# Expert attention on one NeuronCore: the order of a step's projections, the place and form of the routing, the split of the values

## The chip, the cores and the metric

The kernel runs on one core of one Trainium2 chip. The metric is the time of the whole program on the device in microseconds (us), median of the runs.

## What is computed

Eight blocks follow one another, each adding its output to the residual stream of 2 x 1024 tokens by 128 channels. The change concerns the block `_L1_ffn_ref`, which runs twice (stages `g0_` and `g1_`). The reference, cut to it:

```python
def _L1_ffn_ref(x, Wq, Wkv, Ws, Wd, Wo):
    H, E, DH, K = (8, 5, 64, 3)
    ss = sigmoid(x @ Ws).reshape(b, t, H, E);  sd = sigmoid(x @ Wd).reshape(b, t, H, E)
    ms = _topk_mask(ss, K);  md = _topk_mask(sd, K)
    ss_g = ss * ms;  sd_g = sd * md
    q5 = (x @ Wq).reshape(b, t, H, E, DH)
    kv = (x @ Wkv).reshape(b, t, 2, H, E, DH)
    q = einsum('bthed,bthe->bhtd', q5, sd_g)
    k = einsum('bthed,bthe->bhtd', kv[:, :, 0], ss_g)
    v = einsum('bthed,bthe->bhtd', kv[:, :, 1], ss_g)
    attn = softmax(einsum('bhid,bhjd->bhij', q * scale, k), axis=-1)
    out = einsum('bhij,bhjd->bihd', attn, v)
    o5 = einsum('bthd,dm->bthm', out, Wo).reshape(b, t, H, E, DIM)
    return einsum('bthem,bthe->btm', o5, md)
```

Each head's queries, keys and values are sums over five experts weighted by gates; the output of a head is handed to the experts that the mask `md` keeps.

## The kernel before

`expert_attention_stage` walks through 8 units (a pair of heads of one batch entry), each of T = 8 steps: step j handles 128 query rows against 1024 keys for the two heads, so there are STEPS = 64 steps, t = j % T. The five engines each run a list of instructions written out by hand and meet at semaphores; the class `HeadStream` holds what belongs to one step.

In a step TensorE makes the scores of the next step (`scores`, L1505: 4 matmuls of 128 x 512), turns the last 256 columns of head 0's probabilities (`transpose`, L1516) and later subtracts their bf16 part (`subtract`, L1525), and multiplies the probabilities of the step before with the values (`values`, L1546, 24 matmuls of 65 columns for each head, in bf16 parts). Between these it projects tokens for steps to come (`project`, L2292): `beside(k)`, for k = 0, 1, 2, issues two matmuls of 320 columns into the banks 6 and 7, for values (eight steps ahead), queries and keys (eleven ahead). There is only this pair of banks, so `beside` first waits until VectorE has multiplied the products before by the gates (`product_ready`). At t = 2 and 6 TensorE also turns the next unit's queries and keys (`turn`, L2298), and ScalarE places them.

VectorE in a step: the two row maxima (`dve_max`, L1595), three products with the gates (`apply_gates`; L2589 for queries, L2592 for keys and values), two sums over experts (`sum_values`, L2599; `sum_keys`, L2606), and the routing of the step before (`dve_route`): a reciprocal of the row sums (L1602), its product with the mask (`share`, L1604), and the product of outputs and share for 2 heads x 5 experts x 64 (L1608). GpSimd adds what was routed into `z` (`route`, L2479 to L2482) at the end of its step, after the low parts of the probabilities (`pool_lo`, L1582) and the sum over the queries' experts (`sum_queries`, L2491 to L2493). SyncE issues two DMA transposes a step, of the high and the low part (L1591).

At a unit's first step (t = 0) the unit's values are split into two bf16 parts in one piece: ScalarE casts 1040 columns (`act_split_values`, L1614), VectorE subtracts (`dve_split_values`, L1618), before it may write the next unit's values over them.

```python
if j + 1 < STEPS:
    hs.dve_max(dve, j + 1, 0)
beside(0)
if j + 1 < STEPS:
    hs.dve_max(dve, j + 1, 1)
...
beside(1)
if t == 0 and unit:
    hs.dve_split_values(dve, unit)
if j + T < TOTAL:
    sum_values(j + T)
if j:
    route(j - 1)
beside(2)
```

The loop for VectorE stands above. In the first 53 steps of a stage all three projections are there; in steps 53 to 55 only that for values, in the last unit none, and there the results are projected out instead (`turn_out`, `project_out`).

Of the kernel before, what the change touches and what calls it, by code (L numbers as in the profile page):

```python
# [14 lines left out]
ALU = mybir.AluOpType  # L15
# [3 lines left out]
P = 128  # L19
# [1425 lines left out]
class HeadStream:  # L1445
# [8 lines left out]
    def __init__(self, core, ctx, tag, sums):  # L1454
# [16 lines left out]
        self.share = sb("share", [P, 2, 5])  # L1471
# [11 lines left out]
        self.recip_ready, self.share_ready = sem("recip_ready"), sem("share_ready")  # L1483
# [43 lines left out]
    def values(self, pe, j, h):  # L1527
        b = j // self.T % 2
        self.wait_turned(pe, j)
        if h == 0:  # L1530
            pe.wait_ge(self.r_split, j + 1)
            if j:
                pe.wait_ge(self.o_ready, j)
            if j % self.T == 0:
                pe.wait_ge(self.v_split, j // self.T + 1)
# [62 lines left out]
    def dve_route(self, dve, j, kept, added):  # L1598
# [5 lines left out]
        self.nc.vector.tensor_tensor(self.share[:], kept, self.core.col(self.recip[:], 5), ALU.mult).then_inc(self.share_ready, 1)  # L1604
        dve.wait_ge(self.share_ready, j + 1)
        if j >= 2:
            dve.wait_ge(added, j - 1)
        self.nc.vector.tensor_tensor(self.routed[:, j % 2], o[:, :, 0:64].unsqueeze(2).to_broadcast([P, 2, 5, 64]),  # L1608
                                     self.share[:].unsqueeze(3).to_broadcast([P, 2, 5, 64]), ALU.mult).then_inc(self.o_ready, 1)

    def act_split_values(self, act, unit, ready):
# [543 lines left out]
def expert_attention_stage(core, tag):  # L2155
# [10 lines left out]
    with ExitStack() as ctx:  # L2166
# [96 lines left out]
        def _(pe):  # L2263
# [74 lines left out]
            for j in range(STEPS):  # L2338
# [18 lines left out]
                beside(0)  # L2357
# [7 lines left out]
                beside(1)  # L2365
# [7 lines left out]
                beside(2)  # L2373
# [13 lines left out]
        def _(act):  # L2387
# [48 lines left out]
            hs.act_split_values(act, 0, (v_ready, T))  # L2436
            for j in range(STEPS):
# [10 lines left out]
                if t == 0 and unit:  # L2448
                    hs.act_split_values(act, unit, (v_ready, (unit + 1) * T))
# [15 lines left out]
        def _(pool):  # L2465
# [57 lines left out]
            for j in range(STEPS):  # L2523
# [8 lines left out]
                if j:  # L2532
# [4 lines left out]
        def _(dve):  # L2537
# [111 lines left out]
            for tile in range(T, LEAD):  # L2649
# [720 lines left out]
```

## Time and profile before

| | |
|---|---|
| median of 3 runs | 2662.1 us (2661.57 to 2664.65) |
| the profiled execution, its own time | 2660.86 us |
| its span | 2659.0 us |
| PE busy | 2357.8 us (89%) |
| DVE busy | 2034.9 us (77%) |
| ACT busy | 1478.0 us (56%) |
| POOL busy | 1783.3 us (67%) |
| first and last L1559 in g0_ and g1_ (all x256) | 1389.9 to 2630.1 us |

PE is TensorE's matmuls, DVE VectorE, ACT ScalarE, POOL GpSimd. A row of the timeline gives start, duration and instruction, and in brackets how long the engine had been idle before and who ended that. Matmuls are pipelined, so from one group to the next the starts tell what the group costs, and the printed duration is somewhat longer; the same holds for VectorE, whose next instruction starts before the printed end of the last.

### The profile page before, as it was taken

What the parts mean: (1) busy time and instruction counts of PE and PEld (TensorE: products, weight loads), DVE (VectorE), ACT (ScalarE), POOL (GpSimd) and SP (SyncE); (2) the same over time, 40 slices, a digit from 0 to 9 for tenths busy, and PEclk for the clock granted to TensorE, in tenths of its full rate; (3) what the DMA queues carried; (4) which work ended last, traced back from release to release, by engine and by line L of the source; (5) the groups of instructions that cost most, each with busy time, mean ns of one, the idle gap of its engine ahead of it and who ended that gap; (6) DMA issues with size and microseconds to landing.
All of it is one profiled execution on the core that took longest, in us unless ns stands there. A gap on an engine that the chain in (4) does not pass through costs nothing. (4 is left out here: it accounts for less than half of the span.)

```text
span 2659.0 us, 55314 instructions
## 1 busy us (share of the span) xinstructions
PE 2357.8 (89%) x21054; PEld 1521.2 (57%) x21054; DVE 2034.9 (77%) x3668; ACT 1478.0 (56%) x2069; POOL 1783.3 (67%) x1676
## 2 busy tenths in 40 slices
PE   6788777887799999999979999999879799999987
PEld 3555534644466666666655666665634466666655
DVE  7998545545677777777679999998577999999983
ACT  4222122332788888888924556665653255566564
POOL 0888200000899999999947888888710478888885
PEclk9899779988899999999989999999989999999997
DMA  1000000001699998989924656666610256666665
GB/s 45 1 1 0 1 24 14 1 24 53 117 166 148 158 160 151 161 152 154 150 83 87 112 110 114 112 114 118 124 32 0 70 112 112 112 112 115 116 119 107
DMA packets 829351, 243.47 MB, mean 92 GB/s; under 512 B 811528, under 2 KB 820232, under 8 KB 829088
## 3 DMA queue, kind: packets, MB, share of 16 engines
q1 hardware_dynamic: 829088, 239.93, 49.0%
q8 instruction: 168, 2.75, 0.4%
q14 instruction: 95, 0.78, 0.1%
HBM read 20.70 MB, written 1.05 MB: 8 GB/s over the span
## 5 line engine op out<-in xcount | busy, mean ns | idle before, releaser
L2292 PE MATMUL banks<-g_w,normed_t 128*128 128x320 f32 x1536 | 508.3, 457 | 47.8 <-DVE g_scratch L2592 34.0
L1582 POOL TENSOR_TENSOR g_p_lo<-g_p,g_p_hi 128x768 bf16<-128x768 f32 (+1 forms) x256 | 478.2, 1889 | 34.9 <-POOL g_z L2482 22.3
L1775 DVE TENSOR_REDUCE at_negmax<-banks 128x1 f32<-128x1024 f32 x256 | 301.6, 1220 | 152.9 <-PE banks L1687 152.9
L2292 PEld LDWEIGHTS banks<-g_w,normed_t 128*128 128x128 f32 x1536 | 261.6, 189 | 237.6 <-DVE g_scratch L2592 115.0
L1752 POOL TENSOR_TENSOR at_p_lo<-at_p,at_p_hi 128x640 bf16<-128x640 f32 x256 | 356.1, 1408 | 13.4 <-ACT at_p_hi L1740 11.7
L1595 DVE TENSOR_REDUCE g_negmax<-banks 128x1 f32<-128x1024 f32 x256 | 310.1, 1217 | 40.7 <-PE banks L1505 40.5
L1559 ACT ACTIVATE g_p<-banks,g_negmax 128x1024 f32<-128x1024 f32 x256 | 284.9, 1113 | 9.1 <-DVE g_negmax L1595 8.8
L1733 ACT ACTIVATE at_p<-banks,at_negmax 128x1024 f32<-128x1024 f32 x256 | 285.4, 1115 | 6.3 <-DVE at_negmax L1775 6.3
L1687 PE MATMUL banks<-at_k_t,at_q 64*128 64x512 f32 x1024 | 257.0, 620 | 18.1 <-POOL at_k_t L2036 10.0
L1505 PE MATMUL banks<-g_k_t,g_q 64*128 64x512 f32 x1024 | 256.2, 619 | 16.9 <-ACT g_p L1559 10.4
L1572 ACT CAST g_r_hi<-banks 128x256 bf16<-128x256 f32 x128 | 47.6, 372 | 396.5 <-PE banks L1516 396.5
L1566 ACT CAST g_p_hi<-g_p 128x768 bf16<-128x768 f32 (+1 forms) x256 | 241.7, 944 | 6.9 <-DMA g_t_lo<-g_p_lo 2.9
L2592 DVE TENSOR_TENSOR g_scratch<-banks,g_gate 128x640 f32<-128x640 f32 x256 | 209.5, 819 | 5.0 <-PE banks L2292 1.4
L1546 PE MATMUL banks<-g_v_hi,g_t_hi 128*128 128x65 bf16 x1792 | 193.8, 195 | 15.1 <-DMA g_t_lo<-g_p_lo 15.0
L1546 PE MATMUL banks<-g_v_lo,g_t_hi 128*128 128x65 bf16 x1792 | 193.9, 195 | 0.0
L1546 PE MATMUL banks<-g_v_hi,g_t_lo 128*128 128x65 bf16 x1792 | 192.9, 195 | 0.0
L1740 ACT CAST at_p_hi<-at_p 128x640 bf16<-128x640 f32 x256 | 185.9, 726 | 7.7
L1759 POOL TENSOR_TENSOR at_u_lo<-at_u 128x768 bf16<-128x768 f32 x128 | 188.1, 1470 | 2.3 <-ACT at_u L1746 1.6
L1546 PEld LDWEIGHTS banks<-g_v_hi,g_t_hi 128*128 128x128 bf16 x1792 | 167.5, 98 | 34.2 <-DMA g_t_lo<-g_p_lo 20.0
L1546 PEld LDWEIGHTS banks<-g_v_lo,g_t_hi 128*128 128x128 bf16 x1792 | 167.3, 99 | 2.8
L1546 PEld LDWEIGHTS banks<-g_v_hi,g_t_lo 128*128 128x128 bf16 x1792 | 167.5, 99 | 0.0
L1505 PEld LDWEIGHTS banks<-g_k_t,g_q 64*128 64x128 f32 x1024 | 88.8, 187 | 129.3 <-issue 96.0
(419 smaller groups left out, 5996.0 us busy)
## 6 DMA issues: line engine op xcount, KB each, us to landing
at_swapped<-at_crossed SPq DMA_DIRECT2D x128, 128.0 KB, 2.7
g_w<-in_ex_w SPq DMA_DIRECT2D x2, 2880.0 KB, 11.5
f_w<-in_W SPq DMA_DIRECT2D x2, 1024.0 KB, 5.6
at_rope<-in_rope SPq DMA_DIRECT2D x1, 2048.0 KB, 9.6
at_t_hi<-at_p_hi SPq DMA_TRANSPOSE x128, 3.6
at_t_lo<-at_p_lo SPq DMA_TRANSPOSE x128, 3.6
g_t_hi<-g_p_hi SPq DMA_TRANSPOSE x128, 4.2
g_t_lo<-g_p_lo SPq DMA_TRANSPOSE x128, 4.2
```

Source lines behind the costliest of these rows:

```text
L1505: ins = self.nc.tensor.matmul(self.core.ps[2 * h + half], self.q[rows, b, t * P:(t + 1) * P], self.kt[rows, b, half * CHUNK:(half + 1) * C ...
L1546: ins = self.nc.tensor.matmul(self.sums[:, at:at + 65], p, v[:, b, k, h, :], start=(k == 0 and i == 0), stop=(k == self.T - 1 and i == 2))
L1559: self.nc.scalar.activation(self.p[:, j % 2, h, :], self.core.banks[:, 2 * h:2 * h + 2, :], ACT.Exp, bias=self.negmax[:, h:h + 1]).then_in ...
L1566: self.nc.scalar.copy(self.part(self.p_hi, j, h), self.p[:, j % 2, h, 0:self.WIDTH[h]]).then_inc(self.hi_ready, 1)
L1582: self.nc.gpsimd.tensor_tensor(self.part(self.p_lo, j, h), self.p[:, j % 2, h, 0:self.WIDTH[h]], self.part(self.p_hi, j, h), ALU.subtract) ...
L1595: self.nc.vector.tensor_reduce(self.negmax[:, h:h + 1], self.core.banks[:, 2 * h:2 * h + 2, :], AX.XY, ALU.max, negate=True).then_inc(self ...
L1687: ins = self.nc.tensor.matmul(self.core.ps[self.pair(j, h) + half], self.q[rows, b, t * P:(t + 1) * P], self.kt[rows, b, half * CHUNK:(hal ...
L1733: self.nc.scalar.activation(self.p[:, j % 2, h, :], self.core.banks[:, first:first + 2, :], ACT.Exp, bias=self.negmax[:, j % 2, h:h + 1]). ...
L1752: self.nc.gpsimd.tensor_tensor(self.p_lo[:, j % self.RING, h, :], self.p[:, j % 2, h, 0:self.BY_DMA * P], self.p_hi[:, j % self.RING, h, : ...
L1775: self.nc.vector.tensor_reduce(self.negmax[:, j % 2, h:h + 1], self.core.banks[:, first:first + 2, :], AX.XY, ALU.max, negate=True).then_i ...
L2292: nc.tensor.matmul(out[:, 0:ED], core.xt[:, at:at + P], w[:, kind * H + tile // (T * BATCH) * 2 + h, :], start=True, stop=True).then_inc(p ...
L2592: v.tensor_tensor((k_product if kind == 1 else v_product)[:, tile % 2], src.rearrange("p h (c e) -> p h c e", e=E), own.unsqueeze(2).to_br ...
```

## The change

It touches only the two stages of expert attention.

- Projections: `beside(0)` now comes before the scores on TensorE, `beside(1)` behind them, `beside(2)` between the products with the values. On VectorE they stand accordingly: `beside(0)` at the step's start, `beside(1)` between the two maxima, `beside(2)` after them.
- Routing: from j = 2 to j = 56 step j routes step j - 2, right behind `beside(0)`, and GpSimd adds the same step; from j = 56 on step j - 1 is routed at the old place (step 56 does both). `share` is gone: each head is one instruction with a scalar and two tensors, (output x reciprocal) x mask, over 5 x 64.
- Values: split in two halves of four tiles, the first at t = 4 of the unit before, the second at t = 0.

```diff
@@ dve_route @@
-        self.nc.vector.tensor_tensor(self.share[:], kept, self.core.col(self.recip[:], 5), ALU.mult).then_inc(self.share_ready, 1)
-        dve.wait_ge(self.share_ready, j + 1)
         if j >= 2:
             dve.wait_ge(added, j - 1)
-        self.nc.vector.tensor_tensor(self.routed[:, j % 2], o[:, :, 0:64].unsqueeze(2).to_broadcast([P, 2, 5, 64]),
-                                     self.share[:].unsqueeze(3).to_broadcast([P, 2, 5, 64]), ALU.mult).then_inc(self.o_ready, 1)
+        for h in range(2):
+            ins = self.nc.vector.scalar_tensor_tensor(out=self.routed[:, j % 2, h], in0=o[:, h, 0:64].unsqueeze(1).to_broadcast([P, 5, 64]),
+                                                      scalar=self.recip[:, h:h + 1], in1=kept[:, h].unsqueeze(2).to_broadcast([P, 5, 64]),
+                                                      op0=ALU.mult, op1=ALU.mult)
+        ins.then_inc(self.o_ready, 1)
+    def half(self, i):
+        return slice(self.T // 2 * i, self.T // 2 * (i + 1))
+    def act_split_values(self, act, unit, i, ready):
         act.wait_ge(*ready)
         act.wait_ge(self.ones_ready, 1)
-        self.nc.scalar.copy(self.v_hi[:, unit % 2], self.v[:]).then_inc(self.v_split_hi, 1)
+        if unit >= 2:
+            act.wait_ge(self.av_done, 2 * self.T * (unit - 1))
+        self.nc.scalar.copy(self.v_hi[:, unit % 2, self.half(i)], self.v[:, self.half(i)]).then_inc(self.v_split_hi, 1)
+    def dve_split_values(self, dve, unit, i):
+        dve.wait_ge(self.v_split_hi, 2 * unit + i + 1)
+        self.nc.vector.tensor_tensor(self.v_lo[:, unit % 2, self.half(i)], self.v[:, self.half(i)], self.v_hi[:, unit % 2, self.half(i)],
+                                     ALU.subtract).then_inc(self.v_split, 1)
@@ TensorE, step j @@
+                beside(0)
                 if j + 1 < STEPS:
                     hs.scores(pe, j + 1)
-                beside(0)
+                beside(1)
                 hs.transpose(pe, j)
                 if j:
                     hs.values(pe, j - 1, 0)
-                beside(1)
+                beside(2)
                 hs.subtract(pe, j)
                 if j:
                     hs.values(pe, j - 1, 1)
-                beside(2)
@@ ScalarE, step j, behind the cast of head 0's probabilities @@
                 if t == 0 and unit:
-                    hs.act_split_values(act, unit, (v_ready, (unit + 1) * T))
+                    hs.act_split_values(act, unit, 1, (v_ready, (unit + 1) * T))
+                if t == 4 and unit + 1 < UNITS:
+                    hs.act_split_values(act, unit + 1, 0, (v_ready, (unit + 1) * T + T // 2))
@@ GpSimd, end of step j @@
-                if j:
+                if 2 <= j <= STEPS - T:
+                    route(j - 2)
+                if j >= STEPS - T:
                     route(j - 1)
@@ VectorE, step j @@
+                beside(0)
+                if 2 <= j <= STEPS - T:
+                    route(j - 2)
                 if j + 1 < STEPS:
                     hs.dve_max(dve, j + 1, 0)
-                beside(0)
+                beside(1)
                 if j + 1 < STEPS:
                     hs.dve_max(dve, j + 1, 1)
-                beside(1)
+                beside(2)
                 if t == 0 and unit:
-                    hs.dve_split_values(dve, unit)
+                    hs.dve_split_values(dve, unit, 1)
+                if t == 4 and unit + 1 < UNITS:
+                    hs.dve_split_values(dve, unit + 1, 0)
                 if j + T < TOTAL:
                     sum_values(j + T)
-                if j:
+                if j >= STEPS - T:
                     route(j - 1)
-                beside(2)
                 if j + LEAD < TOTAL:
                     sum_keys(j + LEAD)
```

How the instructions now follow one another, at two places. TensorE's queue in the middle of stage g0_, around a step's scores, before (the L1546 rows are products with the values, L2292 the projections, L1505 the scores, L1516 the turned probabilities):

```order
L1546 MATMUL banks<-g_v_hi,g_t_lo 128x65
L2292 MATMUL banks<-g_w,normed_t 128x320 x2
L1505 MATMUL banks<-g_k_t,g_q 128x512 x4
L2292 MATMUL banks<-g_w,normed_t 128x320 x2
L1516 MATMUL banks<-identity,g_p 128x128 x2
L1546 MATMUL banks<-g_v_hi,g_t_hi 128x65
```

What stands in the same queue now is the next piece; nothing between these rows was taken out or put in:

```order
L1545 MATMUL banks<-g_v_hi,g_t_lo 128x65
L2298 MATMUL banks<-g_w,normed_t 128x320 x2
L1504 MATMUL banks<-g_k_t,g_q 128x512 x4
L2298 MATMUL banks<-g_w,normed_t 128x320 x2
L1515 MATMUL banks<-identity,g_p 128x128 x2
L1545 MATMUL banks<-g_v_hi,g_t_hi 128x65
```

The kinds of instruction stand in the same rotation; what moved is which of the three projections sits at which place, and where in the rotation a step begins.

VectorE's queue, one whole rotation from the gates' product for the projection ahead of the scores, before (L2592 and L2589 products with the gates, L2606 keys' sum, L1595 maxima, L2599 values' sum, L1602 to L1608 routing):

```order
L2592 TENSOR_TENSOR g_scratch<-banks,g_gate 128x640
L2606 TENSOR_REDUCE g_tok<-g_scratch 128x128
L1595 TENSOR_REDUCE g_negmax<-banks 128x1
L2592 TENSOR_TENSOR g_scratch<-banks,g_gate 128x640
L1595 TENSOR_REDUCE g_negmax<-banks 128x1
L2589 TENSOR_TENSOR g_scratch<-banks,g_gate 128x640
L2599 TENSOR_REDUCE g_v<-g_scratch 128x2x64
L1602 RECIPROCAL g_recip<-banks 128x2
L1604 TENSOR_TENSOR g_share<-g_mask,g_recip 128x10
L1608 TENSOR_TENSOR g_routed<-banks,g_share 128x640
```

and now (L2603 and L2600 the products with the gates, L1601 and L1606 routing, L1594 maxima, L2610 values' sum, L2617 keys' sum):

```order
L2603 TENSOR_TENSOR g_scratch<-banks,g_gate 128x640
L1601 RECIPROCAL g_recip<-banks 128x2
L1606 SCALAR_TENSOR_TENSOR g_routed<-banks,g_recip,g_mask 128x320 x2
L1594 TENSOR_REDUCE g_negmax<-banks 128x1
L2600 TENSOR_TENSOR g_scratch<-banks,g_gate 128x640
L1594 TENSOR_REDUCE g_negmax<-banks 128x1
L2603 TENSOR_TENSOR g_scratch<-banks,g_gate 128x640
L2610 TENSOR_REDUCE g_v<-g_scratch 128x2x64
L2617 TENSOR_REDUCE g_tok<-g_scratch 128x128
```

The routing and the keys' sum have changed places: the routing now stands ahead of the first maximum and the sum at the end; L1604 is gone, and two instructions of 320 stand for one of 640.

## Rows read from the trace of the kernel before

**Rows 1.** Windows, middle of stage g0_: busy us of each engine, count, PEclk, DMA share, GB/s.

```profile
1680.00:1750.00 70.00, 66.63 (x607) 41.86 (x606) 65.05 (x89) 40.09 (x56) 60.86 (x61) 1.00 0.64 120
```

**Rows 2.** Timeline of ScalarE, one unit of g0_: start us, us, instruction.

```profile
1676.14 0.37 ACT L1572 CAST g_r_hi<-banks 128x256 bf16<-128x256 f32 x1 [3.24 <-PE banks L1516]
...
1685.18 0.37 ACT L1572 CAST g_r_hi<-banks 128x256 bf16<-128x256 f32 x1 [3.61 <-PE banks L1516]
...
1693.35 0.37 ACT L1572 CAST g_r_hi<-banks 128x256 bf16<-128x256 f32 x1 [3.61 <-PE banks L1516]
...
1701.67 0.37 ACT L1572 CAST g_r_hi<-banks 128x256 bf16<-128x256 f32 x1 [2.88 <-PE banks L1516]
...
1740.96 0.37 ACT L1572 CAST g_r_hi<-banks 128x256 bf16<-128x256 f32 x1 [3.24 <-PE banks L1516]
```

**Rows 3.** Timeline of TensorE, step t = 3 of that unit, without L1546.

```profile
1698.15 1.99 PE L1505 MATMUL banks<-g_k_t,g_q 64*128 64x512 f32 x8
1700.07 1.34 PE L2292 MATMUL banks<-g_w,normed_t 128*128 128x320 f32 x4
...
1702.33 1.34 PE L2292 MATMUL banks<-g_w,normed_t 128*128 128x320 f32 x4
...
1704.59 1.34 PE L2292 MATMUL banks<-g_w,normed_t 128*128 128x320 f32 x4
1705.87 1.99 PE L1505 MATMUL banks<-g_k_t,g_q 64*128 64x512 f32 x8
1707.79 1.34 PE L2292 MATMUL banks<-g_w,normed_t 128*128 128x320 f32 x4
```

**Rows 4.** Timeline of VectorE, the same step.

```profile
1700.17 1.23 DVE L1595 TENSOR_REDUCE g_negmax<-banks 128x1 f32<-128x1024 f32 x1 [0.23 <-PE banks L1505]
1701.45 0.82 DVE L2592 TENSOR_TENSOR g_scratch<-banks,g_gate 128x640 f32<-128x640 f32 x1
...
1703.71 0.82 DVE L2589 TENSOR_TENSOR g_scratch<-banks,g_gate 128x640 f32<-128x640 f32 x1 [0.31 <-PE banks L2292]
...
1705.18 0.16 DVE L1602 RECIPROCAL g_recip<-banks 128x2 f32<-128x2 f32 x1
1705.38 0.17 DVE L1604 TENSOR_TENSOR g_share<-g_mask,g_recip 128x10 f32<-128x10 f32 x1
1705.58 0.82 DVE L1608 TENSOR_TENSOR g_routed<-banks,g_share 128x640 f32<-128x640 f32 x1
1706.32 0.81 DVE L2592 TENSOR_TENSOR g_scratch<-banks,g_gate 128x640 f32<-128x640 f32 x1
1707.17 0.82 DVE L2606 TENSOR_REDUCE g_tok<-g_scratch 128x128 f32<-128x640 f32 x1
1707.91 1.22 DVE L1595 TENSOR_REDUCE g_negmax<-banks 128x1 f32<-128x1024 f32 x1
```

**Rows 5.** Timeline of VectorE and line L1618: the split of a unit's values.

```profile
1679.38 1.41 DVE L1618 TENSOR_TENSOR g_v_lo<-g_v,g_v_hi 128x1040 bf16<-128x1040 f32 x1 [0.38 <-ACT g_v_hi L1614]
...
L1618 DVE TENSOR_TENSOR g_v_lo<-g_v,g_v_hi x16: 1242/1419/1580, 1405.1 to 2584.7; 128x1040 bf16<-128x1040 f32 x16
```

**Rows 6.** Lines L1604, L2085 and L1022: ns min/median/max, first and last start, forms.

```profile
L1604 DVE TENSOR_TENSOR g_share<-g_mask,g_recip x128: 170/171/500, 1427.2 to 2645.7; 128x10 f32<-128x10 f32 x128
...
L2085 DVE SCALAR_TENSOR_TENSOR at_crossed<-banks,at_bias,at_rope x64: 736/742/743, 666.1 to 1274.1; 128x512 f32<-128x512 f32 x64
...
L1022 DVE SCALAR_TENSOR_TENSOR residual<-f_y,f_stat,residual x32: 344/347/352, 410.6 to 651.0; 128x128 f32<-128x128 f32 x32
```

**Rows 7.** Timeline of GpSimd: two starts of the routing's first sum.

```profile
1714.45 0.86 POOL L2481 TENSOR_TENSOR g_z<-g_z,g_routed 128x320 f32<-128x320 f32 x1 [0.43 <-DVE g_routed L1608]
...
1722.03 0.86 POOL L2481 TENSOR_TENSOR g_z<-g_z,g_routed 128x320 f32<-128x320 f32 x1
```

**Rows 8.** TensorE's wait in the last unit of g1_, and the window behind it.

```profile
2597.73 0.24 PE L1546 MATMUL banks<-g_v_hi,g_t_hi 128*128 128x65 bf16 x1 [2.99 <-DMA g_t_lo<-g_p_lo]
...
2598.00:2602.00 4.00, 4.00 (x53) 3.71 (x51) 1.14 (x3) 2.81 (x4) 0.63 (x1) 0.50 0.77 145
```

More of the change, by code:

```diff
@@ L1470, in __init__ @@
         self.recip = sb("recip", [P, 2])
-        self.share = sb("share", [P, 2, 5])
         self.routed = sb("routed", [P, 2, 2, 5, 64])
@@ L1482, in __init__ @@
         self.av_done = sem("av_done")
-        self.recip_ready, self.share_ready = sem("recip_ready"), sem("share_ready")
+        self.recip_ready = sem("recip_ready")
         self.o_ready = sem("o_ready")
@@ L1534, in values @@
             if j % self.T == 0:
-                pe.wait_ge(self.v_split, j // self.T + 1)
+                pe.wait_ge(self.v_split, 2 * (j // self.T) + 2)
         at = (j % 2) * 130 + h * 65
@@ L1603, in dve_route @@
         dve.wait_ge(self.recip_ready, j + 1)
-        self.nc.vector.tensor_tensor(self.share[:], kept, self.core.col(self.recip[:], 5), ALU.mult).then_inc(self.share_ready, 1)
-        dve.wait_ge(self.share_ready, j + 1)
         if j >= 2:
             dve.wait_ge(added, j - 1)
-        self.nc.vector.tensor_tensor(self.routed[:, j % 2], o[:, :, 0:64].unsqueeze(2).to_broadcast([P, 2, 5, 64]),
-                                     self.share[:].unsqueeze(3).to_broadcast([P, 2, 5, 64]), ALU.mult).then_inc(self.o_ready, 1)
-    def act_split_values(self, act, unit, ready):
+        for h in range(2):
[6 more added lines that the diff above has]
+    def act_split_values(self, act, unit, i, ready):
         act.wait_ge(*ready)
         act.wait_ge(self.ones_ready, 1)
-        self.nc.scalar.copy(self.v_hi[:, unit % 2], self.v[:]).then_inc(self.v_split_hi, 1)
-    def dve_split_values(self, dve, unit):
-        dve.wait_ge(self.v_split_hi, unit + 1)
-        self.nc.vector.tensor_tensor(self.v_lo[:, unit % 2], self.v[:], self.v_hi[:, unit % 2], ALU.subtract).then_inc(self.v_split, 1)
+        if unit >= 2:
[5 more added lines that the diff above has]
+                                     ALU.subtract).then_inc(self.v_split, 1)
 class TransferStream:
@@ L2435, in _ @@
                 hs.act_hi(act, 0, h)
-            hs.act_split_values(act, 0, (v_ready, T))
+            for i in range(2):
+                hs.act_split_values(act, 0, i, (v_ready, T // 2 * (i + 1)))
             for j in range(STEPS):
@@ L2595, in sum_values @@
             def sum_values(tile):
-                if tile % T == 0 and tile:
-                    dve.wait_ge(hs.v_split, tile // T)
+                if tile % 4 == 0 and tile >= T:
+                    dve.wait_ge(hs.v_split, tile // 4 - 1)
                 dve.wait_ge(product_ready, (last_of(tile, 2) + 1) // 2)
@@ L2654, in _ @@
                 else:
-                    hs.dve_split_values(dve, 0)
+                    for i in range(2):
+                        hs.dve_split_values(dve, 0, i)
                 apply_gates(n + 2, 6)
```

## The prediction

> **What bounds the kernel now.** I read the stage's windows first, then the starts of one unit's steps, then TensorE's and VectorE's timelines of one plain step side by side; the change touches only g0_ and g1_. [...]
>
> Call the projections A (the last before the scores), B (behind the scores), C (between the two products with the values). They share one pair of banks, so each waits for VectorE's gate product of the one before. In the plain step [rows 3, 4] projection B starts at 1700.07, its gates at 1701.45 (1.38 later), C at 1702.33 (0.88 later), its gates at 1703.71, A at 1704.59, the scores at 1705.87 (1.28), the next B at 1707.79 (1.92). That is a closed ring: 1.38 + 0.88 + 1.38 + 0.88 + 1.28 + 1.92 = 7.72 us. B and C are waited for at both ends, and nothing else enters it.
>
> VectorE goes round beside it with little room. Instructions on it follow each other some 0.09 us before the printed end (0.82 printed, next start 0.74 later [rows 4]), so a maximum costs 1.22 - 0.09 = 1.13. From gates C to gates A it takes 2.61 (1703.71 to 1706.32), from gates A to the first maximum 1.59 (to 1707.91), so gates B could start 1706.32 + 1.59 + 1.13 = 1709.04. The ring lets them start at 1707.79 + 1.38 = 1709.17. **The cushion is 0.13 us**: what VectorE is delayed by more than that lengthens the step.
>
> The unit from 1676.14 to 1740.96 takes 64.82 [rows 2], eight plain steps would be 61.76. Of the 3.06 over, 9.04 and 8.17 at t = 0 and 1 make 1.77, the turning at t = 2 and 6 makes 0.60 each (8.32 from 1693.35 to 1701.67; the other is alike), and 0.09 is left. The 1.77 is the split of the values: a wait of 0.38 for ScalarE's cast and 1.41 on VectorE [rows 5], together 1.79 where the cushion is nearly used up.
>
> **The change, part by part.**
>
> *Projections ahead of the scores.* One might expect TensorE to fill a gap here. The order printed above says that its queue is the same rotation as before: projection, scores, projection, turned probabilities, values, projection, values. Only the tile and kind at each place and the name "start of the step" have moved. The new ring is A 1.28, scores 1.92, B to gates 1.38, to C 0.88, to gates 1.38, to A 0.88 = 7.72 [rows 3, 4], the same six terms. From C to the next A TensorE's own work is less than the 2.26 of gates and handover, as it is now. Gain 0; bounds 0.02 either way in a step (the spread that the starts of plain steps show in these rows), 53 x 0.02 = 1 us a stage.
>
> *Routing earlier in the rotation, in two products.* VectorE between gates A and the first maximum: gates 0.74, reciprocal 0.20 (1705.18 to 1705.38), two products. This form of product on 320 columns is not in the trace; on 128 columns it takes 0.347, on 512 0.742 [rows 6], so by the line between them 320 take 0.545, and 0.455 to the next start. Ends: 0.26 (the 128) and 0.655 (the 512); I take 0.455, as the shape lies between. Sum 0.74 + 0.20 + 0.91 = 1.85. The scores are ready 2.02 after their start (1698.15 to 1700.17, where VectorE waited for them [rows 3, 4]), which is 1.28 + 2.02 - 1.38 = 1.92 after gates A. So the maximum waits for TensorE by 0.07, and the routing costs nothing there. Gates B: VectorE could have them 1.85 + 1.13 = 2.98 after gates A, the ring has them at 1.28 + 1.92 = 3.20. **The cushion becomes 0.22.** From gates C to gates A VectorE now has gates, two sums: about 3 x 0.74 = 2.2, against 2.61, and the ring asks 0.88 + 1.38 = 2.26. L1604 goes, 0.17 as a rule and up to 0.50 [rows 6]; such long ones are what I see behind the 0.09 a unit that was left over. With the larger cushion I take this as gone: 7 units x 0.09 = 0.6 us a stage.
>
> *Values in halves.* The half on VectorE: 1.42 for 1040 columns [rows 5]; at the 1.03 ns a column of the two products above (0.395 over 384), 520 take 0.88 at most, and 0.71 if all of it halves; less the overlap, 0.62 to 0.79, I take 0.75. ScalarE's cast stands behind head 0's cast as before, but is half as long, and gates C now end later than it starts; I give that wait 0.05. Gates C to gates A: 2.2 + 0.80 = 3.00, 0.74 beyond the 2.26; less the cushion 0.22 leaves 0.52 for a half. There are 13 of them in a stage beside projections (t = 4 in units 0 to 6, t = 0 in units 1 to 6): 13 x 0.52 = 6.8, where before 6 x 1.77 = 10.6. Gain 3.8 us a stage; with 0.62 and with 0.79 it is 5.5 and 3.2.
>
> *GpSimd.* Its round, once it doesn't wait, is 1722.03 - 1714.45 = 7.58 [rows 7], below 7.72. Its routing was waiting 0.43 for VectorE; routed a step later it doesn't, so it runs ahead and the low parts and their transposes start earlier. Nobody on the ring waits for it: gain 0, and no cost, since 7.58 < 7.72.
>
> *Turning steps* stay at 8.32: TensorE alone sets them, and its work is the same.
>
> *The way out.* Steps 53 to 55 have one projection, which no longer stands between the scores and the turned probabilities that ScalarE copies first; the bounds are 0 and 3 x 1.28 = 3.8. The last split of a unit (step 56) halves too, 0 to 1. In the last unit the routing keeps its place. GpSimd adds two steps' outputs in step 56, ahead of a unit that is bound by its chain. I take 1.2 together, near the lower end, as other chains run beside the projection there.
>
> Sum for a stage: 3.8 + 0.6 + 1.2 = 5.6 us; two stages 11.2. From the profiled execution's 2660.9 this gives 2649.7. The median of the runs is 2662.1, 1.2 above that execution, so **2651**.
>
> [...] The split is the kind of VectorE instruction that reads two tensors from SBUF while GpSimd is nearly always busy. In 16 such instructions the shortest took 1.242 and the longest 1.580 [rows 5], so being held up cost 0.34 at most, and the sum above goes by the median.
> [...]
>
> **Rivals.**
> 1. *The two products are slow, and VectorE becomes the bound (slower).* For: it is an unmeasured size, with a broadcast PSUM operand. Against: the 512 form also reads PSUM, and its 64 executions lie within 0.01 us [rows 6]. It decides from a start-to-start time of (3.20 - 1.13 - 0.94) / 2 = 0.565 on. At 0.655 gates B come 2.25 + 1.13 = 3.38 after gates A, 0.18 late: 53 x 0.18 = 9.5, and no cushion for the halves, 13 x 0.22 = 2.9. Net 12.4 - 5.6 = +6.8 a stage: 2676. From 0.62 on it would be slower by over 0.2%.
> 2. *Each half is held up by GpSimd.* One half gets the whole 0.34 on top: 13 x 0.34 = 4.4 a stage, gain 1.2: 2660, no change. For: the halves meet GpSimd 13 times, not 6. Against: the median lies in the middle of the spread, and part of it is in the sum already.
> 3. *The change doesn't do what it says.* The head of the ring is the same, and if the cushion absorbs nothing, a half costs 0.74: 13 x 0.74 = 9.6 against 10.6. Gain about 1 a stage and the rest nil: 2660.
> [...]
>
> **How the numbers follow.** About 0.2% (5.3 us) is what a measurement of this kernel can tell from no change, so faster means below 2656.8 and slower above 2667.4. My forecast 0.60, with a range of its own of 2645 to 2657 from the bounds of the half and the way out; rival 1 0.10; rival 2 0.09; rival 3 0.10; rival 4 0.11, two thirds of it on the good side. Faster: 0.60 less 0.02, and 0.10 of rival 4: 0.68. Slower: rival 1, and 0.01: 0.11. Same: 0.21. The range runs from rival 4's good end to just above rivals 2 and 3: 2639 to 2662; rival 1 is left out.
>
> **What would show it.** Starts of the first cast of each step (L1571 now): plain steps 7.70 to 7.72; turning steps 8.32; t = 0 and t = 4 with their followers some 0.5 over, and 9.04 nowhere but where VectorE also compares counts. The products L1606 at 0.54 printed, and the first maximum idle by under 0.1 for the scores. GpSimd's wait for the routed product gone up to step 56. I am wrong if plain steps are longer than 7.75 (then look at L1606 and what follows it), or shorter than 7.6 (then the ring isn't what I take it for); if L1623 is far from 0.7 to 0.9; or if the difference lies in the last unit.

## The result and the profile after

The changed kernel takes **2650.35 us** (median of 5 runs, 2645.49 to 2652.14), before 2662.1 (5 runs, 2661.55 to 2664.65): ratio 0.995, 95% interval 0.9935 to 0.9964. Faster by half a per cent, 0.65 us from the 2651.0 predicted and inside the range. The profiled execution took 2652.14 us, its span 2650.4 (before: 2659.0). The median fits better than its terms do, as the rest of this text shows. The two medians differ by 11.75 us, the two profiled executions by 8.6; the account below is of the 8.6.

The window of the same 70 us as in [rows 1], after:

```profile
1680.00:1750.00 70.00, 68.79 (x651) 43.99 (x651) 65.34 (x92) 41.64 (x60) 63.22 (x64) 1.00 0.69 120
```

Every engine is a little fuller, at the same clock. Where the time went is read from the first cast of each step on ScalarE, one unit (before: [rows 2]); columns as there.

```profile
1683.45 0.37 ACT L1571 CAST g_r_hi<-banks 128x256 bf16<-128x256 f32 x1 [3.24 <-PE banks L1515]
1691.16 0.37 ACT L1571 CAST g_r_hi<-banks 128x256 bf16<-128x256 f32 x1 [2.71 <-PE banks L1515]
1699.23 0.37 ACT L1571 CAST g_r_hi<-banks 128x256 bf16<-128x256 f32 x1 [3.60 <-PE banks L1515]
1707.56 0.37 ACT L1571 CAST g_r_hi<-banks 128x256 bf16<-128x256 f32 x1 [2.87 <-PE banks L1515]
1715.27 0.37 ACT L1571 CAST g_r_hi<-banks 128x256 bf16<-128x256 f32 x1 [3.24 <-PE banks L1515]
1722.98 0.37 ACT L1571 CAST g_r_hi<-banks 128x256 bf16<-128x256 f32 x1 [2.71 <-PE banks L1515]
...
1747.09 0.37 ACT L1571 CAST g_r_hi<-banks 128x256 bf16<-128x256 f32 x1 [3.24 <-PE banks L1515]
```

The step lengths are 7.71, 8.07, 8.33, 7.71, 7.71, and so on: 63.64 for the unit, where before took 64.82. Plain steps stayed 7.71. A half of the split costs 0.36 (8.07 - 7.71).

VectorE around such a half, behind the gates of projection C (between the products with the values), with GpSimd's low parts of the probabilities (L1581) beside it:

```profile
1685.49 0.82 DVE L2603 TENSOR_TENSOR g_scratch<-banks,g_gate 128x640 f32<-128x640 f32 x1 [0.30 <-PE banks L2298]
1686.26 0.70 DVE L1623 TENSOR_TENSOR g_v_lo<-g_v,g_v_hi 128x520 bf16<-128x520 f32 x1
1686.32 4.33 POOL L1581 TENSOR_TENSOR g_p_lo<-g_p,g_p_hi 128x768 bf16<-128x768 f32 x2 [0.24 <-POOL g_z L2491]
...
1686.88 0.81 DVE L2610 TENSOR_REDUCE g_v<-g_scratch 128x128 f32<-128x640 f32 x1
1687.61 0.81 DVE L2617 TENSOR_REDUCE g_tok<-g_scratch 128x128 f32<-128x640 f32 x1
1688.33 0.81 DVE L2603 TENSOR_TENSOR g_scratch<-banks,g_gate 128x640 f32<-128x640 f32 x1
```

From gates C to gates A it is 2.84 (1688.33 - 1685.49), of which the half takes 0.62 start to start. The ring asks 2.26, the cushion gives 0.22: 0.36 remains. The sum of the prediction, with one smaller number in it.

That holds from step 20 on. In steps 4, 8, 12 and 16 it doesn't. The same place at step 4 and, in the second piece, step 8:

```profile
1456.38 1.64 POOL L1581 TENSOR_TENSOR g_p_lo<-g_p,g_p_hi 128x768 bf16<-128x768 f32 x1 [0.24 <-ACT g_p_hi L1565]
1456.79 1.78 DVE L1623 TENSOR_TENSOR g_v_lo<-g_v,g_v_hi 128x520 bf16<-128x520 f32 x1
...
1489.49 1.65 POOL L1581 TENSOR_TENSOR g_p_lo<-g_p,g_p_hi 128x768 bf16<-128x768 f32 x1 [0.24 <-POOL g_z L2488]
1489.70 1.99 DVE L1623 TENSOR_TENSOR g_v_lo<-g_v,g_v_hi 128x520 bf16<-128x520 f32 x1
```

GpSimd began 0.41 and 0.21 before VectorE, and the half took 1.78 and 1.99 instead of 0.70. It ends 0.55 behind GpSimd's instruction both times (1458.57 against 1458.02, 1491.69 against 1491.14): **of the 0.70 that it takes alone, 0.55 lies behind the other's end**. In the unit above VectorE came first, by 0.06 us (1686.26, 1686.32), and there the half took its 0.70 and GpSimd's pair 4.33, where such a pair with no half beside it takes 3.73:

```profile
1710.64 3.73 POOL L1581 TENSOR_TENSOR g_p_lo<-g_p,g_p_hi 128x768 bf16<-128x768 f32 x2 [0.24 <-POOL g_z L2491]
```

So it is in both stages: the eight halves of steps 4, 8, 12 and 16 began 0.21 to 0.42 behind GpSimd's low part, took 1.77 to 1.99 and ended 0.55 or 0.56 behind it; the 18 later ones beside projections began 0.04 to 0.08 ahead of it and took 0.70.

In fact the split of the kernel before was held up too, only by a shorter instruction. GpSimd beside the split of [rows 5], a step of its sum over the queries' experts:

```profile
1678.97 0.73 POOL L2491 TENSOR_TENSOR g_scratch<-g_scratch 128x256 f32<-128x256 f32 x1
```

It ended at 1679.70, and the split, begun at 1679.38, ended 1.10 behind it; 14 of the 16 splits ended so, 1.09 to 1.11 behind one of GpSimd's. So 1.42 was not the split's own length; that is the 1.24 of the two shortest, which had no GpSimd instruction beside them, and a half alone takes 0.70.

At step 16 the held-up half sets off a second wait. VectorE's comparison of the counts (L2586) follows there, and now starts behind GpSimd's second low part:

```profile
1558.07 2.12 POOL L1581 TENSOR_TENSOR g_p_lo<-g_p,g_p_hi 128x1024 bf16<-128x1024 f32 x1 [1.05 <-ACT g_p_hi L1565]
1558.96 1.42 DVE L2586 TENSOR_SCALAR g_mask<-g_mask 128x320 f32<-128x320 f32 x1
```

It takes 1.42, where `split_by_phase` below has 0.32 for it. It reads one tensor from SBUF and not two, and it too ends 0.19 behind GpSimd (1560.38, 1560.19). Step 16 is 10.77 long, by phase 7.72.

Two more groups of the profile after, the two lines as min/median/max in ns:

```profile
L1606 DVE SCALAR_TENSOR_TENSOR g_routed<-banks,g_recip,g_mask x256: 540/546/552, 1435.5 to 2638.8; 128x320 f32<-128x320 f32 x128
...
L1623 DVE TENSOR_TENSOR g_v_lo<-g_v,g_v_hi x32: 687/701/1989, 1410.2 to 2584.4; 128x520 bf16<-128x520 f32 x32
```

**The whole account**, in us, by the starts of the steps' first casts (before, after, gain):

| stretch | before | after | gain |
|---|---|---|---|
| span's start to first gates of g0_ (not touched) | 1365.25 | 1370.93 | -5.7 |
| first gates to step 0, g0_ | 50.48 | 51.59 | -1.1 |
| steps 0 to 52, g0_ | 423.32 | 420.03 | 3.3 |
| steps 52 to 56 | 28.44 | 28.32 | 0.1 |
| steps 56 to 63 | 51.41 | 47.60 | 3.8 |
| step 63 of g0_ to step 0 of g1_ | 210.03 | 214.01 | -4.0 |
| steps 0 to 56, g1_ | 451.94 | 448.36 | 3.6 |
| steps 56 to 63 | 51.89 | 46.61 | 5.3 |
| step 63 to the end | 26.22 | 22.90 | 3.3 |
| sum | 2659.0 | 2650.4 | 8.6 |

The stages' middle gives 7 us of the two executions' difference, the two last units 9. The end gives 3.3, some 1.9 of it in TensorE's busy time: its last 136 matmuls took 13.50 at a mean clock of 0.66 before, and 11.58 at 0.78 after. The other 1.4 is time that TensorE waited.

```profile
2632.76:2659.00 26.24, 13.50 (x136) 10.77 (x136) 4.00 (x11) 2.75 (x11) 8.01 (x7) 0.66 0.39 88
```

```profile
2627.46:2650.40 22.94, 11.58 (x136) 9.47 (x136) 3.70 (x11) 2.76 (x11) 7.72 (x7) 0.78 0.44 100
```

The first row is before's, the second after's. The -5.7 lies in stages whose code is the same, and 2.9 of the -4.0 in what stands between step 63 and the first gates of g1_ (159.5 and 162.4). In the traces of all thirteen kernels the same code up to the first gates of g0_ took from 1364.2 to 1370.9, without a pattern that goes with the changes: `products_only`, which differs from before by the two products alone, has 1368.25. So single executions differ by some us there, the kernel after has the longest of them, and the cause stays open. The other 1.1 of the -4.0 is the entry to g1_, as in g0_.

### The profile page after: what moved, and what is told of

Read it like the earlier page. It is cut to its first block and busy times, and to the rows that moved or that the text cites. A ratio compares the mean times of both kernels' runs of the same rounds, so it can differ in the third digit from the quotient of the medians.

```text
span 2650.4 us, 55375 instructions
## 1 busy us (share of the span) xinstructions
PE 2358.9 (89%) x21054; PEld 1523.3 (57%) x21054; DVE 2028.7 (77%) x3684; ACT 1480.5 (56%) x2085; POOL 1781.9 (67%) x1676
## 5 line engine op out<-in xcount | busy, mean ns | idle before, releaser
L1581 POOL TENSOR_TENSOR g_p_lo<-g_p,g_p_hi 128x768 bf16<-128x768 f32 (+1 forms) x256 | 490.0, 1923 | 101.5 <-ACT g_p_hi L1565 75.9
L1594 DVE TENSOR_REDUCE g_negmax<-banks 128x1 f32<-128x1024 f32 x256 | 309.9, 1218 | 35.5 <-PE banks L1504 35.5
L2603 DVE TENSOR_TENSOR g_scratch<-banks,g_gate 128x640 f32<-128x640 f32 x256 | 210.3, 822 | 56.2 <-PE banks L2298 55.2
```

What stands on the lines that cost most here:

```text
L1581: self.nc.gpsimd.tensor_tensor(self.part(self.p_lo, j, h), self.p[:, j % 2, h, 0:self.WIDTH[h]], self.part(self.p_hi, j, h), ALU.subtract) ...
L1594: self.nc.vector.tensor_reduce(self.negmax[:, h:h + 1], self.core.banks[:, 2 * h:2 * h + 2, :], AX.XY, ALU.max, negate=True).then_inc(self ...
L2603: v.tensor_tensor((k_product if kind == 1 else v_product)[:, tile % 2], src.rearrange("p h (c e) -> p h c e", e=E), own.unsqueeze(2).to_br ...
```

## The experiments

Eleven kernels, in three groups, each on one chip beside the kernel before: the first three with `split_by_phase` (before had a median of 2660.74 us there), the two with a third product with `quarters` and `split_behind_sums` (2661.17), `step56_late`, `phase_and_step56` and `quarters_behind_sums` (2661.15). Ratios are to the kernel before; the step times are read from one profiled execution of each.

### One part alone

`halves_only` is the kernel before with the split in halves (the diff of the values above, nothing else). `products_only` is the kernel before with the two products of 320 at the old place. `later_whole` is the kernel after with the whole split at t = 0, on ScalarE as on VectorE:

```diff
-                if t == 0 and unit:
-                    hs.dve_split_values(dve, unit, 1)
-                if t == 4 and unit + 1 < UNITS:
-                    hs.dve_split_values(dve, unit + 1, 0)
+                if t == 0 and unit:
+                    hs.dve_split_values(dve, unit)
```

> The kernel before with the values split by halves, nothing else. Theory (a ring of 7.72 us with a cushion of 0.13 us on VectorE): where a half takes its 0.70 us, t = 0 and t = 4 cost about 0.5 us each instead of 1.77 us at t = 0, so 0.7 us a unit, 5 to 9 us in all by two stages. If halves meet GpSimd's low parts as in the changed kernel (1.8 to 2.0 us instead of 0.70), each such one takes 1.1 to 1.3 us of it back, and the time is the one before. Rival (the routing's new place is what pays, the halves nothing): no change within 2 us.

> The kernel before with the routing in one product per head and without the share, at its old place. Theory: on VectorE 0.20 us and the share's long ones go, 0.17 us comes (two times 0.455 for 0.74); plain steps stay 7.71 since the ring sets them, only the 7.8 us steps go to 7.71. Gain 1 to 2 us in all. Rival (VectorE's total work sets the step): the 0.03 us a step are seen too, 3 to 5 us.

> The changed kernel, values split in one piece at t = 0. Theory: VectorE is late by 1.41 us and the wait for the cast (0.3 to 0.4) less the cushion 0.22, so t = 0 with the step behind it costs 1.5 to 1.6 us over 2 x 7.71, against 0.36 twice in the changed kernel where the halves aren't held up, and 0.36 to 1.45 where they are. Time 3 to 6 us above the changed kernel, that is 2653 to 2656 us. Rival (GpSimd holds up a whole split as it does a half): the long ones reach 2.5 us and more, and the kernel is as slow as before or slower. In the last unit, which has no split of its own after step 56, it shows whether that unit's gain of 4 to 5 us a stage came with the routing (then it stays) or with the halves (then it goes).

Measured: halves alone 2658.01 (10 runs), ratio 0.9994 (0.9985 to 1.0004); products alone 2658.92 (10 runs), 0.9992 (0.9981 to 1.0003); everything but the halves 2661.91 (10 runs), 1.0009 (0.9998 to 1.0021). **No part alone can be told from no change**; together they give 0.5%. The expectations of 5 to 9 us for the halves alone and of 2653 to 2656 for the whole split missed; for the latter the rival came. The steps show why. With halves alone a late unit takes 64.22 at the least (before 64.82), t = 0 and 1 at 7.90 and 8.17; seven of its 26 halves beside projections took 1.15 to 1.23. With the products alone the odd steps of 7.8 go to 7.71, and 9.01 and 8.17 stay. With the order but the split whole, t = 0 and 1 are 9.57 and 8.44, longer than before: now each split meets GpSimd. Its line, and one of them with the instruction of GpSimd that came before it:

```profile
L1618 DVE TENSOR_TENSOR g_v_lo<-g_v,g_v_hi x16: 1243/2223/2373, 1409.2 to 2591.7; 128x1040 bf16<-128x1040 f32 x16
```

```profile
1683.91 1.64 POOL L1581 TENSOR_TENSOR g_p_lo<-g_p,g_p_hi 128x768 bf16<-128x768 f32 x1 [0.24 <-POOL g_z L2482]
1684.30 2.35 DVE L1618 TENSOR_TENSOR g_v_lo<-g_v,g_v_hi 128x1040 bf16<-128x1040 f32 x1 [0.38 <-ACT g_v_hi L1614]
```

The median rose from 1.419 [rows 5] to 2.223: what stands right ahead of the split on GpSimd is now a low part of 1.64, no longer the sum's 0.73. With the products alone it is still 1.40, so the new order does it; that it is the later routing, which GpSimd no longer waits for, is argued, since no run moves the routing without the projections. The split ends 1.10 behind GpSimd's (1686.65, 1685.55), as its own 1.24 would less the 0.14 that the halves too show.

The last units (steps 56 to 63) take 48.1 and 48.8 in this kernel, 49.8 and 48.8 with the products alone, 46.1 and 51.0 with the halves alone, and took 51.4 and 51.9 before. So with the new order they are some 3 us shorter even without the halves; but kernels that keep the old order differ among themselves by as much, and these traces don't show what brings it.

### Where the halves stand

`split_by_phase` puts the halves up to step 16 behind the keys' sum, where GpSimd's first low part is over; `split_behind_sums` puts all there.

```diff
-                if t == 0 and unit:
-                    hs.dve_split_values(dve, unit, 1)
-                if t == 4 and unit + 1 < UNITS:
-                    hs.dve_split_values(dve, unit + 1, 0)
...
                 if j + LEAD < TOTAL:
                     sum_keys(j + LEAD)
+                split_half()
```

Here `split_half` holds the four lines taken out; by phase the last line stands under `if j <= 2 * T`, and for later steps the four lines stay where they were.

> [...] Theory (a half that starts after GpSimd's low part has begun waits until that is done): the four halves take 0.70 us instead of 1.77 to 1.99, steps 4, 12 and their followers cost 0.36 over instead of 1.45, 1.1 us for each of four halves, 4 us a stage, 8 us in all: 2642 us. Rival (the long halves have another cause, such as the place in the program or the first units' gates): their length stays at 1.7 to 2.0 us and the time within 2 us of the changed kernel.

> The changed kernel with every half behind the keys' sum. In steps up to 16 as in split_by_phase: 0.70 us each. [...] Time between 2638 (all follow the first part) and 2675 us (9 a stage behind both). Rival (the place behind the sums is what helps): all halves at 0.70 us and 2638 us.

Measured: by phase 2637.81 (6 runs), 0.9919 (0.9905 to 0.9933); all behind the sums **2631.16** (4 runs, 2630.3 to 2633.73), 0.9888 (0.9874 to 0.9901). Each moves nothing but one instruction on one engine. The second lies below both its expectation and its rival (2638 and more). Step 4 of the second, VectorE and GpSimd:

```profile
1455.11 1.65 POOL L1581 TENSOR_TENSOR g_p_lo<-g_p,g_p_hi 128x768 bf16<-128x768 f32 x1 [0.24 <-ACT g_p_hi L1565]
1455.48 0.81 DVE L2610 TENSOR_REDUCE g_v<-g_scratch 128x128 f32<-128x640 f32 x1
1456.21 0.81 DVE L2617 TENSOR_REDUCE g_tok<-g_scratch 128x128 f32<-128x640 f32 x1
1456.93 0.69 DVE L1623 TENSOR_TENSOR g_v_lo<-g_v,g_v_hi 128x520 bf16<-128x520 f32 x1
```

The sums (one input each) run beside the low part at their usual 0.81; the half starts when it is over (1456.76) and takes 0.69. Steps 4 and 5, with their followers at 8, 12 and 16, were 8.44 + 8.43 and more; here 7.71 + 8.04. To the start of the last unit the stage takes 448.35 after, 442.04 by phase, 443.43 with all behind the sums (late units 63.87 instead of 63.65: there GpSimd's first low part ends just after the half has begun, and it takes 0.838 at the median). Its last units are shorter: 44.57 and 44.56, no step over 6.84, where by phase they were 47.6 and 46.6. That is 2.3 us for both stages together; the medians differ by 6.7, but the profiled execution of `split_by_phase` was the fastest of its six (2632.26), so the rest isn't seen in these traces. With all behind the sums the halves from step 20 on took 0.83 to 0.85 and that of step 56 1.19: no run shows the 9 us a stage by which the expectation comes to 2675.

Step 16 fell from 10.77 to 7.72 in both, since the comparison of the counts took 0.32 again:

```profile
1547.09 0.69 DVE L1623 TENSOR_TENSOR g_v_lo<-g_v,g_v_hi 128x520 bf16<-128x520 f32 x1
1547.70 0.32 DVE L2586 TENSOR_SCALAR g_mask<-g_mask 128x320 f32<-128x320 f32 x1
```

The rows are from `split_by_phase`; GpSimd's second low part began at 1547.93, behind the start of L2586. Of the 6.6 us that steps 0 to 52 lost by the held-up halves (420.03 against 413.48), step 16 with its follower makes 2.95, the other three 1.1 to 1.3 each.

### The ring and the cushion

One product of 320 more in the routing of either kernel, its result unused (nothing is left out):

```diff
         dve.wait_ge(self.recip_ready, j + 1)
+        self.nc.vector.scalar_tensor_tensor(out=self.unused[:], in0=o[:, 0, 0:64].unsqueeze(1).to_broadcast([P, 5, 64]),
+                                            scalar=self.recip[:, 0:1], in1=kept[:, 0].unsqueeze(2).to_broadcast([P, 5, 64]),
+                                            op0=ALU.mult, op1=ALU.mult)
```

> The kernel before with one more product of 320 columns in each routing (its result is not used; nothing is left out), 0.455 us more on VectorE between gates C and gates A. Theory: cushion 0.13, so plain steps go from 7.71 to 7.71 + 0.455 - 0.13 = 8.04; if VectorE had no cushion 8.17; if TensorE alone set the step 7.71.

> The changed kernel with the same further product (result not used, nothing left out), now between gates A and the first maximum. Theory: cushion 0.22 (0.06 to the scores, the rest behind them), so plain steps go from 7.71 to 7.71 + 0.455 - 0.22 = 7.95; without a cushion 8.17.

One run each: 2692.78 and 2699.52 us. Plain steps (t = 4 and 5) of before with it, then one (t = 3) of after with it, on ScalarE:

```profile
1718.46 0.37 ACT L1573 CAST g_r_hi<-banks 128x256 bf16<-128x256 f32 x1 [3.35 <-PE banks L1517]
1726.50 0.37 ACT L1573 CAST g_r_hi<-banks 128x256 bf16<-128x256 f32 x1 [3.56 <-PE banks L1517]
1734.53 0.37 ACT L1573 CAST g_r_hi<-banks 128x256 bf16<-128x256 f32 x1 [3.56 <-PE banks L1517]
```

```profile
1713.96 0.37 ACT L1572 CAST g_r_hi<-banks 128x256 bf16<-128x256 f32 x1 [3.12 <-PE banks L1516]
1721.93 0.37 ACT L1572 CAST g_r_hi<-banks 128x256 bf16<-128x256 f32 x1 [3.49 <-PE banks L1516]
```

8.04 and 8.03 (7.71 + 0.455 - 0.13), and 7.97 (7.71 + 0.455 - 0.22 = 7.95). **The ring and both cushions are shown** by these steps, to 0.02 us. In the kernel before the steps right behind a turning step (t = 3 and 7) took only 7.83 and the turning steps 8.72, so the 0.33 isn't paid alike in all; in the kernel after, turning steps took 8.57, which is 0.25 more, like the plain ones. The kernel after pays more in total, since its halves beside projections are now all held up (1.47 to 1.65):

```profile
L1627 DVE TENSOR_TENSOR g_v_lo<-g_v,g_v_hi x32: 689/1634/1650, 1405.1 to 2628.7; 128x520 bf16<-128x520 f32 x32
```

### The last unit

`step56_late` is the kernel after with the half of step 56 alone behind routing and sums; `phase_and_step56` has both moves (`if j <= 2 * T or j == STEPS - T`).

> The kernel after, with one half alone moved: that of step 56 stands behind the routings and sums instead of ahead of them. Theory (step 55's routing, which frees z for GpSimd and with it the low parts of the last unit, stood behind the half, and the two DMA waits of the last unit come from that): the last unit falls to some 44.6 us as with all halves behind the sums, from 47.6 and 46.0, without a step over 7.0; steps 0 to 52 unchanged, 448.4 to the start of the last unit; 2 to 3 us a stage, 2644 to 2647. Rival (the last unit's length is luck of the transposes, and the halves' place in the units before sets it): 46 to 52 us again, with a step over 7.5 somewhere, 2650 +- 4.

> Both moves: halves of the first three units (steps up to 16) and that of step 56 behind the keys' sum, all others ahead of the sums. Theory (the two costs are separate and add): 442.0 to the last unit as with the halves by phase, 44.6 in the last unit as with all behind the sums: 2638 - 2 x 3 = some 2631 to 2633, equal to all behind the sums (2631) or just below. Rival (the last unit's waits hang on the state that the units before leave, as VectorE and GpSimd stand to each other): the last unit stays at 47 to 48, 2637.

Step 56 of the kernel after, VectorE and GpSimd:

```profile
1874.47 0.70 DVE L1623 TENSOR_TENSOR g_v_lo<-g_v,g_v_hi 128x520 bf16<-128x520 f32 x1 [1.93 <-ACT g_v_hi L1619]
1875.09 0.16 DVE L1601 RECIPROCAL g_recip<-banks 128x2 f32<-128x2 f32 x1
1875.29 1.01 DVE L1606 SCALAR_TENSOR_TENSOR g_routed<-banks,g_recip,g_mask 128x320 f32<-128x320 f32 x2
...
1876.38 0.86 POOL L2490 TENSOR_TENSOR g_z<-g_z,g_routed 128x320 f32<-128x320 f32 x1 [3.78 <-DVE g_routed L1606]
```

and the same with all halves behind the sums:

```profile
1866.76 1.01 DVE L1606 SCALAR_TENSOR_TENSOR g_routed<-banks,g_recip,g_mask 128x320 f32<-128x320 f32 x2
1868.08 1.19 DVE L1623 TENSOR_TENSOR g_v_lo<-g_v,g_v_hi 128x520 bf16<-128x520 f32 x1 [0.31 <-ACT g_v_hi L1619]
...
1867.85 0.86 POOL L2490 TENSOR_TENSOR g_z<-g_z,g_routed 128x320 f32<-128x320 f32 x1 [2.08 <-DVE g_routed L1606]
```

In the first, VectorE sits idle 1.93 for ScalarE's cast of the values (L1619, behind a cast of the probabilities), with the routing of step 55 queued behind it, and GpSimd waits 3.78 for that, with the low parts of the next step behind. In the second the routing goes first. The low part's transpose is late for TensorE in the first:

```profile
1886.41 0.20 PE L1545 MATMUL banks<-g_v_hi,g_t_hi 128*128 128x65 bf16 x1 [1.90 <-DMA g_t_lo<-g_p_lo]
...
1901.04 0.20 PE L1545 MATMUL banks<-g_v_hi,g_t_hi 128*128 128x65 bf16 x1 [1.43 <-DMA g_t_lo<-g_p_lo]
```

Measured: step 56 alone 2645.94 (4 runs), 0.9940 (0.9924 to 0.9957); both moves 2633.33 (4 runs, 2631.97 to 2635.98), 0.9897 (0.9882 to 0.9911). The step t = 2 fell from 7.67 and 7.60 to 6.38 and 6.42, as the theory says; the later one (8.06 at t = 4, 7.14 at t = 3) stayed, 8.24 and 7.13. TensorE's waits in g0_:

```profile
1881.95 0.20 PE L1545 MATMUL banks<-g_v_hi,g_t_hi 128*128 128x65 bf16 x1 [0.61 <-DMA g_t_lo<-g_p_lo]
...
1896.75 0.20 PE L1545 MATMUL banks<-g_v_hi,g_t_hi 128*128 128x65 bf16 x1 [1.61 <-DMA g_t_lo<-g_p_lo]
```

So my theory holds for one of the two waits, 1.1 to 1.2 us a stage of the 2 to 3 expected, and the times of the kernels don't resolve that. With both moves the last units take 44.6 and 45.7, and the second wait is gone from g0_ and at 0.80 in g1_. What decides the second wait isn't settled: it depends on how the stage was entered, and I have no run that moves it alone.

### Quarters

`quarters` splits at t = 2, 4, 6 and 0, up to step 16 behind the sums and later ahead of them; `quarters_behind_sums` has all behind.

```diff
-        return slice(self.T // 2 * i, self.T // 2 * (i + 1))
+        return slice(self.T // 4 * i, self.T // 4 * (i + 1))
...
+                if t in (2, 4, 6) and unit + 1 < UNITS:
+                    hs.dve_split_values(dve, unit + 1, t // 2 - 1)
```

> split_by_phase with the values split by quarters, at t = 2, 4, 6 of the unit before and at t = 0 (each behind the sums up to step 16, ahead of them after). A quarter takes about 0.38 us on VectorE, 0.30 from start to start. Theory (ring 7.72, of which gates C to gates A 2.26; cushion 0.22): VectorE then needs 2.2 + 0.35 = 2.55 in that stretch, 0.29 late, 0.07 over the cushion, and nothing at t = 2 and 6, where TensorE turns tokens and VectorE has 0.6 to spare. The 13 halves at 0.36 us (4.7 us a stage) become 13 quarters at 0.07 (0.9): 3.8 us a stage, 7.6 in all, 2630 us against 2637.8 of split_by_phase. Rival (each further instruction meets GpSimd's low parts anew): quarters of 1.0 to 2.0 us instead of 0.38 in the trace, the time 2638 us or more.

> The values split by quarters (two tiles each, at t = 2, 4, 6 and 0), all behind the keys' sum. Theory (there the halves of all units were not held up, 0.33 to 0.47 over a plain step, and VectorE's cushion of 0.22 is there anew in each step): a quarter is some 0.42 us printed, 0.35 of VectorE; at t = 4 and 0 it costs 0.07 to 0.15, at t = 2 and 6 nothing beside the turning: a unit 63.1 to 63.3 us instead of 63.7, some 3 us a stage, 2625 to 2628. Rival (a quarter meets GpSimd's instructions oftener and is held up as the quarters ahead of the sums were, 1.4 us and more): steps of 8.2 to 8.4 in the later units, 2645 and more.

Measured: 2666.2 (10 runs), 1.002 (1.001 to 1.003), where 2630 was expected and the rival came, and 2634.66 (4 runs), 0.9901 (0.9886 to 0.9916). Ahead of the sums nearly each quarter is held up; one of 0.42 takes 1.50:

```profile
1698.75 1.65 POOL L1581 TENSOR_TENSOR g_p_lo<-g_p,g_p_hi 128x768 bf16<-128x768 f32 x1 [0.24 <-ACT g_p_hi L1565]
1699.18 1.50 DVE L1623 TENSOR_TENSOR g_v_lo<-g_v,g_v_hi 128x260 bf16<-128x260 f32 x1
```

Behind the sums those at t = 2 and 6 aren't, and take 0.42 (but for step 54's in each stage, 1.75 and 1.74, begun 0.19 behind GpSimd's low part); but in the late units those at t = 4 and 0 still are, by GpSimd's first low part:

```profile
1678.81 3.92 POOL L1581 TENSOR_TENSOR g_p_lo<-g_p,g_p_hi 128x768 bf16<-128x768 f32 x2 [0.24 <-POOL g_z L2491]
1679.95 0.79 DVE L1623 TENSOR_TENSOR g_v_lo<-g_v,g_v_hi 128x260 bf16<-128x260 f32 x1
```

The first of GpSimd's pair, 1.65 long, ends at 1680.46 and the quarter at 1680.74, so it takes 0.785 at the median there, nearly the half's 0.838 at the same place. That is why so little is won: steps of 8.13 in place of 8.19 (0.06, and the two instructions differ by 0.05), and against it the quarters at t = 2 and 6 make the turning steps 8.39 instead of 8.32. A unit is 63.9 against 63.87; expected was 63.1 to 63.3. The cost of a late split behind the sums is thus hardly its own length, but the end of GpSimd's instruction.

## Why the prediction was right, and where it wasn't

- *What bounds the kernel*: right. Plain steps 7.71 after as before, with the same six terms. VectorE's first maximum follows gates A by 1.91 in most steps (predicted 1.92) and by 1.85 in two of a unit, so its wait for the scores is 0.06 at most. The third product lengthened the steps shown above as computed.
- *The products*: right. 0.546 printed (0.545 by the line between the two sizes) and 0.46 to 0.47 from the first's start to the second's (0.455); rival 1 did not come.
- *Values in halves*: the mechanism right, the term mis-sized on both sides. Taken 0.75 + 0.05 for ScalarE, measured 0.62 and no wait: 0.36 instead of 0.52 for a half. Against it stand four halves a stage (steps 4, 8, 12, 16) at 1.77 to 1.99. Rival 2 had this mechanism but priced it from the spread of [rows 5] at 0.34, at every half. It was 1.1 to 1.3 at four of 13, and at one of these, step 16, another 1.1 by the instruction behind it. **The step that failed is the price**: the prediction took 1.42 for the split's own length, where it was 1.24 and a hold-up by GpSimd's short instructions; the long one had never stood ahead of it, and the change moved it (by the new order) to just there. The splits of before never waited as long as a whole long instruction of GpSimd's (1.24 to 1.58 against its low parts of 1.64), and that proved nothing. (At 0.79 for a half the prediction's own sum gives 3.3, not 3.2.)
- *Gain of steps 0 to 52*: 3.3 and 3.5 a stage, predicted 4.4 (3.8 and 0.6). Without the held-up halves it is 9.8 (by phase: 413.48 against 423.32), more than the 4.4: 2.1 of that is 13 x 0.16, and some 2.7 that before's units 1 and 2 took longer at t = 0 and 1 than the unit of [rows 2] (18.52 and 18.62 for both steps, not 17.2), where I had counted 6 equal splits. The comparison of the counts was held up in the kernel before as well: it took 1.52 in each of the two units, and 0.32 to 0.36 by phase, which is 2.4 of the 2.7 if all of it lies on the path. The prediction named it as an exception and gave it no term; 0.6 stays unassigned.
- *The way out*: predicted 1.2, measured 0.1 in steps 52 to 56; and the entry, which the prediction didn't cost, takes 1.1 more in each stage, as by the order one projection more (1.28) now stands ahead of the first turned probabilities.
- *GpSimd, gain 0 and no cost*: right for the ring, wrong in what it set off. Its sum of the routed product (L2481 before, L2490 after) waited for VectorE 76 times of 96 before and 16 times of 96 after, those all from step 56 on; and its long instruction, the low part of 1.64, met the halves.
- *The last unit*: the sum had nothing for it; only rival 4, a last unit that falls differently, had something, at 0.11, and the range goes down to its good end, 2639. No run shows by itself what one wait gone is worth. What the runs show: in the last unit of g1_ TensorE's longest wait for the transposed low parts was 1.84 instead of 2.99 [rows 8], and in the 4 us behind it (2596.50 to 2600.50) the clock was 1.00, not 0.50. The last units became shorter by 3.8 and 5.3, and with it came 3.3 at the end, together more than the middle gave. I had said that the forecast was wrong "if the difference lies in the last unit"; by that test it is half wrong. The total came out by luck: these gains, which the sum didn't hold, stood in for those that the held-up halves took, for the way out and the entries, and for what was lost outside the stages.

A version that beats both kernels is `split_behind_sums`, 2631.16 us, 1.1% below before; `phase_and_step56` and `quarters_behind_sums` lie within its interval.

## What to carry to other kernels

Before moving work, list which instructions of VectorE can be held up (here the subtraction of two tensors in SBUF, a half of it 1.77 to 1.99 instead of 0.70, and the comparison L2586 with one, 1.42 instead of 0.32) and where GpSimd's long ones then start; the price of a meeting was here the rest of GpSimd's instruction less 0.15 (a half that began 1.23 before the low part's end took 1.08 more), whatever the spread of the old order says, and moving one instruction by 1.5 us brought more here than the whole change. Put such an instruction behind ones that aren't held up, here the sums (0.81 beside the low part), check what follows it, and check each phase of the stage, since an order of 0.06 us decided who waited. And cost the stage's ends apart from its middle: the last seven steps of the two stages gave more of the difference between these two executions than the 56 before them.

## What I had not expected of the hardware

- VectorE's half and GpSimd's low part held each other up, whichever was first: halves of 0.70 took 1.78 and 1.99, each ending 0.55 behind GpSimd; GpSimd's pair took 4.33 for 3.73 when VectorE was first by 0.06.
- In the kernel before the split was held up as well, in 12 of 16 executions by a GpSimd instruction of 0.73 and in two by one of 0.46, and ended 1.10 behind it; nothing in its median of 1.419 shows that.
- The sums with one SBUF input took 0.81 beside GpSimd's subtraction as without it (0.801 to 0.820 in 256 executions). A TENSOR_SCALAR with one SBUF input (L2586) didn't escape: 1.42 behind GpSimd's low part, 0.32 ahead of it.
- A product with a scalar and two tensors, one of them in PSUM, took 0.540 to 0.552 on 320 columns in 256 executions, most beside GpSimd's work; none was held up.
